# Feed-forward of a tile two iterations later, with written-out orders before and after a shorter loop

## What is computed

```python
x = x + tanh(g_xattn[0]) * xattn(layernorm(x), ctx, ctx, Wq, bq, Wk, bk, Wv, bv, Wo, bo)   # 16 heads of 16
x = x + tanh(g_ffn[0]) * ffn(layernorm(x), w_gate, w_up, w_down)                            # 256 -> 704 -> 256
def fp4_quant_dequant(x):            # blocks of 16 along the last axis
    scale = max(max(|block|) / 6, 1e-12)
    return GRID[searchsorted(MID, |x / scale|)] * sign(x) * scale
def fp4_linear(x, w): return einsum('bsk,nk->bsn', fp4(x), fp4(w))
ffn = fp4_linear(silu(fp4_linear(x, w_gate)) * fp4_linear(x, w_up), w_down)
```

## Time and profile before

| what | value |
|---|---|
| median of 3 executions | 315.74 us (315.04 to 316.67) |
| the profiled execution, own time | 318.12 us |
| its span | 316.1 us |
| PE busy | 282.2 us (89%) |
| DVE busy | 245.5 us (78%) |
| ACT busy | 165.2 us (52%) |
| POOL busy | 132.3 us (42%) |
| mean granted clock of TensorE | 0.922 |

### The profile page before, as it was taken

The page is one execution under the profiler, slowest core; times in us unless marked ns, Lnnn a source line. Parts: engine busy times, 40 slices in busy tenths (PEclk is TensorE's granted clock), DMA queues, the critical chain, the costliest instruction groups (busy, mean ns, idle before and its releaser), DMA issues.

```text
span 316.1 us, 5634 instructions
## 1 busy us (share of the span) xinstructions
PE 282.2 (89%) x1634; PEld 246.9 (78%) x1634; DVE 245.5 (78%) x706; ACT 165.2 (52%) x532; POOL 132.3 (42%) x161
## 2 busy tenths in 40 slices
PE   2779587796999999999999999999999999995846
PEld 2449586696989989898989898989898988774734
DVE  1977988949488888888888888988898887968471
ACT  1137665555356565665656666656565656513120
POOL 0596434304326454545444444444444444332300
PEclk9997587787599999999999999999999999979697
DMA  4990000000000000000000000000000000000000
GB/s 111 347 326 2 1 1 0 0 2 0 2 2 18 2 17 19 1 17 0 17 0 17 0 17 0 17 0 17 0 20 0 19 1 17 18 1 18 0 17 17
DMA packets 9048, 8.50 MB, mean 27 GB/s; under 512 B 1580, under 2 KB 8775, under 8 KB 9031
## 3 DMA queue, kind: packets, MB, share of 16 engines
q1 hardware_dynamic: 7255, 7.50, 7.4%
q10 hardware_dynamic: 1776, 0.79, 0.9%
HBM read 6.19 MB, written 2.10 MB: 26 GB/s over the span
## 4 chain that ended last, share of the span: by engine, by line
PE 57%; DVE 13%; issue 12%; POOL 11%; ACT 3%; DMA 2%; SPq 1%; POOLq 0%; DVEq 0%; ACTq 0%
PE psT L1121 9%; PE psO L1097 9%; PE psO L1105 9%; PE psG L1006 6%; PE psG L1007 5%; PE psG L1008 5%; PE psO L1147 3%; PE psO L1114 3%; PE psS L1006 2%; POOL ha L976 2%; PE psS L1008 2%; PE psS L1007 2%; DMA X<-in_x 2%; POOL rstd L924 2%; POOL hq L979 2%
## 5 line engine op out<-in xcount | busy, mean ns | idle before, releaser
L402 ACT ACTIVATE probs<-psS,negmax 128x77 f32<-128x77 f32 x256 | 62.2, 331 | 12.8 <-DVE negmax L620 12.6
L1105 PE MATMUL psO<-wdT,hT 128*128 128x256 f32 x192 | 47.4, 397 | 2.9 <-ACT hT L520 2.9
L1097 PE MATMUL psO<-vblk,pT 128*128 128x51 f32 x320 | 43.4, 288 | 1.2 <-ACT pT L437 1.2
L1097 PEld LDWEIGHTS psO<-vblk,pT 128*128 128x128 f32 x320 | 42.7, 211 | 1.7 <-ACT pT L437 1.7
L976 POOL TENSOR_TENSOR ha<-hc,ha 128x704 f32<-128x704 bf16 x15 | 24.3, 1622 | 46.4 <-DVE ha L664 46.4
L1105 PEld LDWEIGHTS psO<-wdT,hT 128*128 128x128 f32 x192 | 35.0, 196 | 10.4 <-ACT hT L509 3.3
L1006 PE MATMUL psG<-wgh,xqh 128*128 128x512 f32 (+1 forms) x96 | 41.9, 436 | 0.9 <-DVE xql L795 0.9
L1007 PE MATMUL psG<-wgl,xqh 128*128 128x512 f32 (+1 forms) x96 | 37.5, 391 | 0.0
L1008 PE MATMUL psG<-wgh,xql 128*128 128x512 f32 (+1 forms) x96 | 37.3, 388 | 0.0
L420 ACT ACTIVATE th<-psG 128x256 f32<-128x256 f32 (+1 forms) x48 | 17.8, 371 | 32.4 <-PE psG L1008 32.4
L628 DVE SCALAR_TENSOR_TENSOR tg<-th,psG 128x256 f32<-128x256 f32 (+1 forms) x48 | 19.1, 398 | 19.9 <-ACT th L420 19.6
(11 more groups left out here) (116 smaller groups left out, 653.7 us busy)
## 6 DMA issues: line engine op xcount, KB each, us to landing
out_x<-X SPq DMA_DIRECT2D x16, 128.0 KB, 1.7
X<-in_x SPq DMA_DIRECT2D x2, 512.0 KB, 10.0
wraw<-in_L_ffn_w_down SPq DMA_DIRECT2D x1, 704.0 KB, 9.9
wraw<-in_L_ffn_w_gate ACTq DMA_DIRECT2D x1, 640.0 KB, 8.9
wraw<-in_L_ffn_w_up SPq DMA_DIRECT2D x1, 640.0 KB, 8.6
X<-in_x SPq DMA_DIRECT2D x4, 128.0 KB, 6.7
X<-in_x SPq DMA_DIRECT2D x2, 256.0 KB, 9.2
vblk<-in_vmask SPq DMA_DIRECT2D x2, 255.0 KB, 7.9
```

Source lines behind the costliest of these rows:

```text
L402: ins = act.activation(probs[:, p, hd * S:(hd + 1) * S], psS[g % 2][:, k * S:(k + 1) * S], ACT.Exp, bias=negmax[:, p, hd:hd + 1])
L1097: ins = pe.matmul(psO[1][:, at:at + SLOTS * VW], pT[:, p, c * P:(c + 1) * P], vblk[:, p, c, :], start=(c == 0), stop=(c == SC - 1), skip_g ...
L1105: return pe.matmul(psO[1][:, 0:D], hT[:, p, c * P:(c + 1) * P], wdT[:, c, :], start=(c == first), stop=(c == last))
```

## The change

`LAG = 2` puts parts (3) and (4) of a tile two iterations later: iteration i now does gate and up of tile i-4, the down projection of tile i-5 and the store of tile i-6. Attention keeps its place. The loop shrinks to iterations 7 to 12 (`FIRST_LOOP, TRIPS = 7, 3`). What stood in `iteration` for i up to 6 and from 13 on is now two lists, `head()` and `tail()`, written out on each engine in an order of their own. The head still contains gate and up of tiles 0, 1, 2 and the down projection of tiles 0, 1 as before, and two more tiles of attention (5 and 6). The tail has the attention of tiles 13 to 15 as before, and the feed-forward of tiles 9 to 15 (before: 11 to 15, and the down projection of 10).

Further: a `scores` matmul waits for `q_hi` alone, the second for `q_lo` too, and the low part of the keys comes last (three matmuls in the order high-high, query low, key low). `gate_up` waits for `c_hi`, and for `c_lo` only ahead of its last two matmuls. `values` waits for each of the three copies of the transposed probabilities at the chunk that needs it. `probs_T` part 1 waits for a new semaphore `s_px`, raised by the exponential of the head that ends at column 1024. The last tile is done in three parts (256, 256, 192 columns), split into `last_scale` and `last_round`, and tiles 13 and 14 transpose `hq` into the banks of the scores, which are free by then.

```diff
 XQ_AT = 7
-FIRST_LOOP, TRIPS = 5, 4
+LAG = 2
+FIRST_LOOP, TRIPS = 7, 3
...
-        def run(eng, iteration):
-
-            for i in range(-1, FIRST_LOOP):
-                iteration(i, i % 2)
+        def run(iteration, eng):
+
             with eng.Fori(0, TRIPS) as t:
                 iteration(2 * t + FIRST_LOOP, FIRST_LOOP % 2)
                 iteration(2 * t + FIRST_LOOP + 1, (FIRST_LOOP + 1) % 2)
-            for i in range(FIRST_LOOP + 2 * TRIPS, TILES + 4):
-                iteration(i, i % 2)
+
+        Z_BANKS = (psT[0], psT[1], psS[1])
+
+        def hidden_banks(n):
+
+            return (psS[1], psS[0]) if just(n, LAST - 2) or just(n, LAST - 1) else (psT[1], psT[0])
...
             def scores(n, p, g):
-                if g == 0:
-                    done(pe, q_lo, KC, n)
-                    if just(n, p):
-                        pe.wait_ge(s_kh, p + 1)
-                        pe.wait_ge(s_kl, p + 1)
+                k, at = g // 2, (g % 2) * GW
+                if g % 2 == 0:
+                    done(pe, q_hi, KC, n, k + 1)
...
+                pe.matmul(o, qh[:, p, k], hi, start=True, stop=False)
+                if g % 2 == 0:
+                    done(pe, q_lo, KC, n, k + 1)
+                pe.matmul(o, ql[:, p, k], hi, start=False, stop=False)
...
             def gate_up(n, p, j):
                 if j == 0:
-                    done(pe, c_lo, 1, n)
+                    done(pe, c_hi, 1, n)
...
+                if j == 0:
+                    done(pe, c_lo, 1, n)
+                for k in range(KC):
+                    ins = pe.matmul(o, xql[:, p, k], wgh[:, k, at:at + w], start=False, stop=(k == KC - 1))
...
             def values(n, p, c0, c1):
 
                 for c in range(c0, c1):
+                    if c % 4 == 0:
+                        done(pe, b_pTs, 3, n, c // 4 + 1)
...
+                xn_T(i + 1, pq)
+                probs_T(i - 1, pb, 1)
+                scores(i, ps, 0)
+                scores(i, ps, 1)
+                probs_T(i - 1, pb, 2)
+                q_proj(i + 1, pq)
+                values_a(i - 1, pb)
+                x_T(i - 2 - LAG, pc)
+                values_b(i - 1, pb)
+                scores(i, ps, 2)
+                gate_up(i - 2 - LAG, pc, 0)
+                att_T(i - 1, pb)
+                gate_up(i - 2 - LAG, pc, 1)
+                attention_out(i - 1, pb)
+                scores(i, ps, 3)
+                probs_T(i, ps, 0)
+                hidden_T(i - 3 - LAG, pd, 0)
+                gate_up(i - 2 - LAG, pc, 2)
+                hidden_T(i - 3 - LAG, pd, 1)
+                down_all(i - 3 - LAG, pd)
...
+            head()
+            run(iteration, pe)
+            tail()
```

More of the change, by code:

```diff
@@ L522, in _ @@
-            act.wait_ge(l_bq, 16)
-            run(act, iteration)
+                x_magic(i - 2 - LAG)
+                xn_out(i + 1, pq)
+                probs_out(i - 1, pb, 1)
+                probs_out(i - 1, pb, 2)
+                exps(i, ps, 0)
+                q_rounded(i + 1, pq)
+                h_magic(i - 3 - LAG, pd)
+                x_hi(i - 2 - LAG, pc)
+                exps(i, ps, 1)
+                tanh(i - 2 - LAG, pc, 0)
+                att_out(i - 1, pb)
+                exps(i, ps, 2)
@@ L526, in _ @@
+            head()
+            run(iteration, act)
+            tail()
         @block.vector
@@ L903, in _ @@
-            dve.wait_ge(l_kmask, 16)
-            keys(0)
-            weights_scale(0)
-            dve.wait_ge(l_bq, 16)
-            run(dve, iteration)
+                residual_out(i - 4 - LAG)
+                maxima(i, ps, 0)
+                maxima(i, ps, 1)
+                x_add(i - 2 - LAG)
+                norm_q_stats(i + 2, ps)
+                x_sub(i - 2 - LAG)
+                norm_q_mean(i + 2, ps)
+                x_quant(i - 2 - LAG, pc)
+                q_rest(i + 1, pq)
+                x_lo(i - 2 - LAG, pc)
@@ new lines, in iteration @@
+                h_floor(i - 3 - LAG, pd)
+                att_norm(i - 1, pb)
+                h_add(i - 3 - LAG, pd)
+                norm_q_apply(i + 2, ps)
+                gated(i - 2 - LAG, pc, 0)
+                maxima(i, ps, 2)
+                hidden(i - 2 - LAG, pc, 0)
+                h_max(i - 2 - LAG, pc, 0)
+                gated(i - 2 - LAG, pc, 1)
+                x1_sum(i - 1, pb)
+                hidden(i - 2 - LAG, pc, 1)
+                maxima(i, ps, 3)
+                x1_stats(i - 1 - LAG, pb)
@@ L910, in _ @@
+            head()
+            run(iteration, dve)
+            tail()
         @block.gpsimd
@@ L1002, in _ @@
+            head()
+            run(iteration, pool)
+            tail()
         @block.tensor
         def _(pe):
-            def mm3(o, ah, al, bh, bl, first, last):
-                pe.matmul(o, ah, bh, start=first, stop=False)
-                pe.matmul(o, ah, bl, start=False, stop=False)
-                return pe.matmul(o, al, bh, start=False, stop=last)
-            pe.wait_ge(l_ctx, 16)
-            pe.wait_ge(l_ident, 16)
-            for k in range(KC):
-                for b in range(B):
-                    at = (k * B + b) * S
-                    ins = pe.transpose(psT[0][:, at:at + S], ctxs[:, b, k * P:(k + 1) * P], ident[0:S, 0:S])
@@ L1116, in attention_out, with x_T @@
                 ins.then_inc(b_wo, 1)
[L1118 to L1122 removed]
+            def x_T(n, p):
+                done(pe, b_q, 1, n)
+                if just(n, LAST):
+                    done(pe, c_lo, 1, n - 1)
+                else:
+                    free(pe, (b_pTs, 3, n + 1 + LAG, 2), (d_hTs, 2, n - 2, 2))
+                turn(psT[0], xq[:, p], KC).then_inc(c_xT, 1)
```

1658 lines of the change are left out of this document (1181 added, 477 removed).

## The result

The changed kernel takes 298.91 us (median of 4 executions, 298.84 to 299.91), the kernel before beside it on the same chip 316.21. The ratio is 0.947, 95% interval 0.943 to 0.951. On two other chips, later, the same kernel took 296.23 (ratio 0.939, 0.934 to 0.943) and 295.31 (0.932, 0.920 to 0.944).

What follows compares the result with a forecast made beforehand. The prediction took PE to bound the loop, with gaps to fill only in head and tail. Head 110, loop 91 and tail 94 made a span of 295 us; predicted median 295, with 286 to 306 holding some 0.8.

Steps and rivals of the forecast that it cites:

- The loop: Six looped iterations, PE full: 15.17 us each with 0.07 for added waits, 91.0 us; bounds 88.9 to 93.
- The head: Stage before the loop: two more attention tiles, half of 26.6 us of PE loss remaining (13.3), so 110 us.
- If nothing found a gap: Head and tail if moved work filled no gap: head 123.2 us, tail 101.7, whole 315.5 against 316.1.
- The tail: Stage after the loop: 71.8 us to the last gate and up matmul, 8.5 lost, 13.9 behind it: 94 us.
- the end chain: Tail from the last gate and up matmul to the end of the span: 13.9 us, against 16.4 before.
- The port rival: Tail: DVE's two-input operations held up by POOL's, a quarter of 40 waiting 0.8 us: 303 us, chance 0.16.
- The interlock rival: Head and tail: PE and DVE don't interlock, 20 of 26.6 us of head loss remain: 304 us, chance 0.14.
- everything fits: Only 7 of 26.6 us lost in head, 4 in tail: 283 us, or 289 with one alone; chance 0.15.
- The clock: Head: PE stands repeatedly, its clock falls, about 35 us of work at half clock: 322 us, slower; chance 0.03.
- nothing: Whole kernel: what is filled in one stage is lost in the other, 316 us; chance 0.02.
- The work at full clock: Head of the kernel before from 20 us on: PE busy 77.01 us times clock 0.81, 62.4 us.
- Signs: Profile if right: DVE over 85% busy in head and tail, iteration 7's first transpose at 106 to 114 us.

Runs made afterwards that it cites:

- after_again: The change run again without any edit, on a third chip: 295.31 us, ratio 0.932 to the kernel before.
- genhead: The change with its written-out head replaced by the loop's iteration written out (general order), tail kept: 315.15 us, ratio 0.999 to the kernel before.
- lag2_gen: The change with both head and tail replaced by the loop's iteration written out (general order), lag of 2 kept: 333.11 us, ratio 1.052 to the kernel before.
- gentail: The change with its written-out tail replaced by the loop's iteration written out (general order), head kept: 313.14 us, ratio 0.992 to the kernel before.
- whole_c: The change with only `gate_up` put back to waiting for its whole operand, on a fourth chip: 301.17 us, ratio 0.957 to the kernel before.
- after_rep: The change run again without any edit, on a second chip: 296.23 us, ratio 0.939 to the kernel before.

## Why the prediction was right, and which steps were not

The forecast was 295 (286 to 306); the change took 298.91, and 296.23 and 295.31 on the later chips. The total holds, and in part by luck: two errors in the tail offset each other by half, and the head fits only a slow start.

- **The loop**, 91.0: measured 90.65, with PE busy for 89.39 of it. That lag and waits are worth nothing there is shown by twelve further runs, all from 90.2 to 91.0. The 0.07 us per iteration for the added waits is below what they tell.
- **The head**, 110: measured 110.4, but 104.2 and 105.0 in the other runs of the same kernel. From 20 us on the loss was to be half of before's, 13.3. PE was busy for 86.63 of 90.41 us; against 76.6 of work at full clock that is 13.8 lost, 3.8 idle and 10.0 to the rate. In after_again (85.04 long) it is 8.4. So the size fits the first run only because its start was slow, and that is luck. The sign for it, a granted clock above 0.9, came true in the record (0.98) but not in the work: 76.6 us of work in 86.63 busy is 0.88. The mechanism, other tiles' scores in front of the places where PE stood, holds: PE's listed waits there fell from 12.0 us to 3.6, and with the general order (genhead) the head is 126.7.
- **"If nothing found a gap"**, 123.2 for the head and 101.7 for the tail: I used these as upper bounds, and they are not. With the general order and the lag the head is 126.6 and the tail 114.8. In the tail the step left out that an iteration without attention does not cost its PE work (7.69 us) but its chain from DVE's rounding to PE (14.2 to 14.7 us in lag2_gen). Why the head is over its bound is not shown. My expectations for lag2_gen and gentail, both too low, come from the same mistake; that for genhead was too low as well.
- **The tail**, 94: measured 96.3. The last gate and up matmul came 78.2 us into it, forecast 80.3: the loss before it was 6.4, not 8.5. **The mis-sized term is the end chain, 18.2 for 13.9.** By the rows: from this matmul's end (279.24) DVE is still busy with tile 14's `ha` until 280.42 (1.2, not priced); `gated` and `hidden` 1.2; the `last_scale` 4.6 (forecast 4.0; one row of 1.30 for 0.42 beside POOL); tile 13's residual 0.4; `last_round` 3.6 (3.75); then 4.6 to the last residual, for which I had 2.0, and 2.6 (2.7) to the end. In those 4.6 us PE first finishes tile 14's down projection, late by 2.2 and slow, and then does twelve matmuls of the last tile and not two chunks. I had taken PE as free there.
- **The port rival**, 303 at 0.16: the mechanism and its count are real, what it was to cost is not. In the tail ten DVE operations with two SBUF inputs take 0.3 to 1.25 us longer than their lone twins, 8.4 us together, just the quarter of 40 at 0.8 us that the rival has; `xa` has a mean of 0.91 and `xneg` of 0.63, so the sign named for it came true for `xa`. But before's tail already held 3.2 us of the kind, within its 61.2, and the tail came to 96 and not 102: "nothing absorbs it" was wrong. Moving 3.4 us of it earned 2.7 in the profiled tail. And `xneg` in the earlier trace rows ended 0.28 us after POOL's operation, not with it.
- **The interlock rival** (304) and **everything fits** (283, 289): neither stage was as long as 117 or as short as 89.7, though a head of 104.2, the price of the second, was seen. **The clock** (322) and **nothing** (316): before's lower level came back in the general order of the tail (0.90), but in the head of the change it cost 10.0 us at most. Two readings behind the clock rival are wrong. It sets 28.5 us, which is busy time at the lower level and so about 15 us of work at full clock, against 29 us of work. And in the first of the three slow stretches PE had not stood just before the clock fell: it was busy throughout from 22 to 28 us, and its 3.2 us of standing lie inside the stretch.
- **The work at full clock**, 62.4: it multiplies by the granted clock, which in before too reads 1.00 from 22 to 24 us while matmuls of 308 columns start 0.26 us apart. By an estimate from that stretch (21.2 to 24.8 us) the 62.4 is up to 2 us too high.
- **Signs**: DVE was to be over 85% busy in head and tail. It was 89% in the tail, but 80% in the head and 84% from 20 us on. The start of iteration 7 (106 to 114 us) holds for the first run alone.
- **Unpriced**: the split waits. I called them worth nothing where PE is full, which is so, and then gave them no term in head and tail. They carry 9.9 us there. The total could still come out right because I took the gap filling as a whole, whatever fills it.

## What to carry to other kernels

Moving work into the ramps of a pipeline pays only if the ramps get an order of their own: here the longer lag alone cost 17 us, and with two written-out orders and split waits lag and all gained as much (written-out orders without a lag were not tried). Price an iteration that lacks a part by the chain it exposes, and not by the work that is left in it: here 14 us and not 7.7. Waits split by operand were worth nothing in the full loop or with the general order, and 10 us once the order had been packed, so try them last and don't judge them alone.

## What the runs showed of the hardware

PE's rate and the granted clock of the records disagree at the start. In the first run of the change the record says 1.00 from 22 to 44 us, with PE busy throughout:

```profile
22.00:44.00 22.00, 22.00 (x115) 21.97 (x114) 15.21 (x29) 10.88 (x35) 8.99 (x10) 1.00 0.07 22
```

The matmuls of 308 columns there start 0.25 us apart. In after_again, the same kernel, the same ones start 0.14 us apart; first the change, then after_again:

```profile
25.34 4.34 PE L1609 MATMUL psG<-vs,rows 77*128 77x48 f32 x20
...
30.13 0.46 PE L1658 MATMUL psS<-kl,qh 128*128 128x308 f32 x1
30.38 0.46 PE L1652 MATMUL psS<-kh,qh 128*128 128x308 f32 x1
...
40.95 1.04 PE L1623 MATMUL psG<-ident,wraw 128*128 128x128 f32 x8
```

```profile
24.25 2.66 PE L1609 MATMUL psG<-vs,rows 77*128 77x48 f32 x20
...
27.24 0.31 PE L1652 MATMUL psS<-kh,qh 128*128 128x308 f32 x1
27.39 0.30 PE L1655 MATMUL psS<-kh,ql 128*128 128x308 f32 x1
```

The spacing doubles, as between the two levels of 1.2 and 2.4 GHz. Equal groups of matmuls tell where the rate changes. Twenty matmuls with `rows` take 4.34 us in the first run, and in after_again 2.66 and then, from 28.11 us, 2.33: there the half rate ends at about 25 us. Eight transposes of `wraw` take 1.04 us in both runs (1.97 in before at 36.19 us, where the clock is 0.50): in the first run the half rate has ended by 40.95 us. From the first scores of tile 0 to the third of tile 1 the first run takes 22.1 us (21.93 to 44.05), after_again 17.8 (20.84 to 38.67), whole_c and gentail 22.1 and 22.3, after_rep 17.9. So the long half rate costs about 4.3 us of the head, more than most edits above; another 1.1 us of the first run's 110.41 is that its first scores begin later.

Behind this first stretch record and spacing agree. In after_again the record falls to 0.50 from 32 to 35 us and again at 46, where the spacing is 0.26 us:

```profile
45.60:47.20 1.60, 1.60 (x9) 1.60 (x8) 1.50 (x6) 1.60 (x7) 0.57 (x2) 0.50 0.00 0
```

In the first run it does so from 51 to 54 us, after PE had stood for most of 48 to 50. What decides how long the first half rate lasts is open, and in that stretch only the spacing shows it.
